# Weights and rows prepared before the barrier between passes, and a bias taken off TensorE in the last graph pass

## The reference, cut to what matters

```python
u = h @ h.T / sqrt(D);  a = softmax(u);  delta = a * adj
attn = delta / (sum(delta) + 1e-10)
hl, hs, hr = h @ wl.T + b_l, h @ ws.T + b_s, h @ wr.T + b_r
ctx = (attn * upper) @ hl + diag(attn)[:, None] * hs + (attn * lower) @ hr
h = relu(layernorm(ctx) * g + beta)
```

## Time and profile before

| | |
|---|---|
| time, median of three runs | 2734.35 us |
| time of the profiled execution | 2734.95 us |
| its span, first to last instruction | 2733.2 us |
| mean granted TensorE clock | 0.964 |
| TensorE busy | 2471.4 us, 90% |
| VectorE, GpSimd, ScalarE busy | 73%, 72%, 62% |

### The profile page before, as it was taken

How to read it: one execution, slowest core, us unless ns; L and a number is a source line. 1 busy time by engine, 2 the same in 40 slices (tenths; PEclk the granted TensorE clock), 3 DMA queues, 4 the chain that set the end, 5 groups by cost and what they waited for, 6 DMA issues and landing times. The chain is left out here.

```text
span 2733.2 us, 65211 instructions
## 1 busy us (share of the span) xinstructions
PE 2471.4 (90%) x21554; PEld 2108.1 (77%) x21554; DVE 1992.3 (73%) x3475; ACT 1689.4 (62%) x3606; POOL 1969.1 (72%) x2189
## 2 busy tenths in 40 slices
PE   6999999985999999869999968888885999999997
PEld 4888888874877777758888857777774888888886
DVE  4777777773677667668888858888787577777776
ACT  4667666664777777745454445555654576666665
POOL 3888788873777777756666647777775588878786
PEclk9999999997999999979999989999997999999998
DMA  7222223115233332172333163333324222232211
GB/s 128 62 71 70 70 65 73 44 50 101 69 84 80 79 81 67 55 129 63 75 73 69 39 120 75 92 79 79 79 70 91 53 69 71 68 72 68 59 46 50
DMA packets 320602, 200.71 MB, mean 73 GB/s; under 512 B 243426, under 2 KB 320484, under 8 KB 320484
## 3 DMA queue, kind: packets, MB, share of 16 engines
q1 hardware_dynamic: 320484, 199.21, 31.6%
HBM read 136.22 MB, written 62.91 MB: 73 GB/s over the span
## 5 line engine op out<-in xcount | busy, mean ns | idle before, releaser
L1179 PE MATMUL l_ps_h<-l_w,l_hT 128*128 128x384 f32 x3456 | 672.0, 347 | 2.3 <-issue 2.3
L457 PE MATMUL l_ps_p<-l_xT,l_w 128*128 128x512 f32 x2304 | 598.3, 407 | 83.3 <-POOL l_xT L379 76.8
L1179 PEld LDWEIGHTS l_ps_h<-l_w,l_hT 128*128 128x128 f32 x3456 | 614.9, 193 | 63.3 <-issue 54.0
L457 PEld LDWEIGHTS l_ps_p<-l_xT,l_w 128*128 128x128 f32 x2304 | 426.3, 191 | 179.8 <-DVE l_w L733 51.7
L784 DVE TENSOR_REDUCE l_st<-l_pr 128x12 f32<-128x768 f32 x192 | 182.9, 953 | 348.7 <-ACT l_pr L663 348.7
L396 POOL TENSOR_TENSOR l_pr<-l_sc,l_st 128x768 f32<-128x768 f32 x192 | 285.1, 1485 | 172.2 <-DVE l_st L777 172.2
L1261 ACT ACTIVATE l_hlr<-l_ps_h 64x384 f32<-64x384 f32 x512 | 248.8, 486 | 196.8 <-PE l_ps_h L1179 190.0
L354 POOL TENSOR_TENSOR v<-v,l_bvs 128x768 f32<-128x768 f32 x192 | 356.2, 1855 | 0.0
L1106 POOL TENSOR_TENSOR l_hlr<-l_hlr,l_sides 128x768 f32<-128x768 f32 x128 | 246.7, 1928 | 125.6 <-ACT l_hlr L1261 125.4
L451 PE MATMUL l_ps_p<-l_w,l_xT 128*128 128x384 f32 x1584 | 312.6, 342 | 15.7 <-ACT v L622 14.8
L451 PEld LDWEIGHTS l_ps_p<-l_w,l_xT 128*128 128x128 f32 x1584 | 272.6, 188 | 25.3 <-ACT v L622 18.8
(11 more groups left out here) (138 smaller groups left out, 4383.6 us busy)
## 6 DMA issues: line engine op xcount, KB each, us to landing
rows<-l_yo SPq DMA_DIRECT2D x256, 192.0 KB, 1.9
l_xa<-rows SPq DMA_DIRECT2D x256, 192.0 KB, 4.3
l_xr<-rows SPq DMA_DIRECT2D x192, 192.0 KB, 2.4
l_xa<-in_x SPq DMA_DIRECT2D x64, 192.0 KB, 4.3
l_xr<-in_x SPq DMA_DIRECT2D x64, 192.0 KB, 2.3
out<-l_yo SPq DMA_DIRECT2D x64, 192.0 KB, 1.9
l_edge<-in_adj SPq DMA_DIRECT2D x80, 128.0 KB, 2.4
raw<-in_L_gnn_Wq SPq DMA_DIRECT2D x12, 144.0 KB, 4.9
```

What stands on the lines that cost most here:

```text
L457: last = nc.tensor.matmul(bank[:, :], W[m][:, l, t, o * P:(o + 1) * P], rows[:, r, t, :], start=c + t == 0, stop=c == 2 and t == KT - 1)
L1179: last = nc.tensor.matmul(ps_h[m][:, :D], hT[gpar][:, l, t, s * P:(s + 1) * P], W[m][:, r, t, :], start=c + t == 0, stop=not (ends and m = ...
```

## The change

1. Weights, row buffers and their semaphores are shared by the passes. A `Feed` object tells each pass where in the running counts it begins. In the last group of an attention pass, or over the last two groups of a graph pass, the streams also turn and split the next pass's 9 weight tiles; the rows of the next pass's first two groups (`g` = 16 and 17) are loaded and turned as if the loop went on, as far as its lookahead reaches. The first graph pass writes into a second set of weight tiles. l0 still prepares its own at its start.
2. The buffer of turned rows in attention passes is doubled.
3. In l0 and l3 the minimum comes after `low_part`.
4. In l1 one VectorE instruction takes the place of the three of ScalarE that normalise a row.
5. The second graph pass does SELF as the first does (`by_matmul = False`), and its stream has `attention` step 3 first in unit 3.

```diff
@@ attention_pass, VectorE
                 nc.vector.tensor_reduce(st[b][:, 0, :], sc[b][:, :, :], AX.X, ALU.max).then_inc(dve_mx, 1)
+
+            def softmax_min(n, s):
+                b = s % 2
                 if wo:
                     nc.vector.tensor_reduce(st[b][:, 1, :], sc[b][:, :, :], AX.X, ALU.min).then_inc(dve_mn, 1)
...
+            def normed(n, count, b):
+                if not inside(n, units) or wo:
+                    return
+                dve.wait_ge(pool_rs, n + 1)
+                dve.wait_ge(dve_mv, n + 1)
+                if counted(16 * count):
+                    dve.wait_ge(s_out[b], 16 * count)
+                nc.vector.tensor_scalar(yo[b][:, :], res[b][:, :], ln[b][:, 6:7], ln[b][:, 9:10], ALU.subtract,
+                                        ALU.mult).then_inc(ready_y, 1)
...
                     softmax_max(n, par, s)
                     low_part(n - 2, s % 2)
+                    softmax_min(n, s)
+                    normed(n - 3, count, 1 - s % 2)
                     if s == 2:
                         edges(i + 1, pair + (1 if par else 0), 1 - par)
                     softmax_sum(n, s)
                     for t in ((0, 1), (2,), (), ())[s]:
                         rows_turned(i + 2, par, t)
+                    if nxt and isinstance(i, int) and i == groups - 1:
+                        if s:
+                            for step in range(KT * (s - 1), KT * s):
+                                weight_low(nxt, step, next_bank(step))
+                        else:
+                            dve.wait_ge(act_v, units)
+                        if s < 3:
+                            for step in range(KT * s, KT * (s + 1)):
+                                weight_turned(nxt, step, next_bank(step), 3)
...
@@ digcn_pass
+    by_matmul = False
...
+        def next_step(i, s):
+
+            j = (i - groups + 2) * UNITS + s if isinstance(i, int) else -1
+            return () if j < 0 else (7, 8) if j == 7 else (j,)
...
@@ digcn_pass, ScalarE
                     left_right(n, b, RIGHT)
+                    for step in next_step(i, s):
+                        weight_high(step)
                     standardise(n - 2, b)
                     normed(n - 4, pair * 4 + 2 * par + s // 2 - 2, b)
-                    if ends:
+                    if by_matmul:
                         act.wait_ge(pe_h, 3 * n + 3)
...
@@ digcn_pass, VectorE
+                    for step in next_step(i, s - 1) if s else next_step(i - 1, UNITS - 1):
+                        weight_low(step)
+                    if s == 3:
+                        attention(i + 1, 1 - par, 3)
+                    itself(n - 1, 1 - b)
                     if ends:
                         context(n - 1, *before)
-                    itself(n - 1, 1 - b)
                     if s == 3:
-                        attention(i + 1, 1 - par, 3)
                         attention(i + 1, 1 - par, 4)
...
                         rows_turned(i + 2, par, s - 2)
+                    for step in next_step(i, s):
+                        weight_turned(step)
...
+    feeds = [Feed(0, x, w0, True, shared.W, 0, 0, 0), Feed(1, kept[0], w1, False, shared.W, 1, 6, 6),
+             Feed(2, kept[1], w2[0], True, shared.W, 1, 6, 6), Feed(3, kept[2], w2[1], True, None, 2, 5, 3),
+             Feed(4, kept[3], w3, True, shared.W, 3, 5, 3)]
```

More of the change, by code:

```diff
@@ L185, in attention_pass @@
         a = Pass(nc, ctx, tag)
-        W = [a.sb(f"w{m}", [P, 2, KT, D], F32R) for m in range(NM)]
+        W = me.W
+        rb, wb = me.rows_base, me.w_base
         ident, raw, s_raw = shared.ident, shared.raw, shared.s_raw
@@ L647, in _ @@
                     rows_high(1, 1, pos - 2)
-            for step in range(3 * KT, steps):
-                weight_high(step)
+            if wo:
+                for t in range(KT):
+                    output_weight_high(t)
             def probs_T(n, b):
@@ L676, in normed @@
             def normed(n, count, b):
-                if not inside(n, units):
+                if not inside(n, units) or not wo:
                     return
@@ L855, in _ @@
             edges(0, 0, 0)
-            for step in range(3 * KT, steps):
-                weight_low(step)
+            if wo:
+                for t in range(KT):
+                    output_weight_low(t)
             ni = [0]
@@ L907, in digcn_pass @@
         loaded = list(shared.loads)
[L908 to L909 removed]
+        own = None if by_matmul else a.sb("own", [P, D])
+        if by_matmul:
             pick = shared.pick
@@ L1412, in itself @@
             def itself(n, b):
-                if ends or not inside(n, units):
+                if by_matmul or not inside(n, units):
                     return
@@ L1471, in inner_norm @@
                                                op0=ALU.mult, op1=ALU.add).then_inc(dve_o, 1)
-            if ends:
+            if by_matmul:
                 nc.vector.memset(bias[:, :].bitcast(F32), 0.0).then_inc(c_zero, 1)
-            weights(LEFT)
             dve.wait_ge(c_mask, masks)
-            for t in range(KT):
-                rows_turned(0, 0, t)
-            weights(RIGHT)
-            attention(0, 0, 0)
-            weights(SELF)
-            for step in range(1, 5):
+            for step in range(5):
                 attention(0, 0, step)
-            rows_turned(1, 1, 0)
-            rows_turned(1, 1, 1)
             dve.wait_ge(s_small, 16 * n_small)
-            if ends:
-                dve.wait_ge(act_w, steps + 1)
+            if by_matmul:
+                dve.wait_ge(c_row, 2)
                 nc.vector.tensor_tensor(bias[32:33, :], brow[32:33, :], bround[32:33, :].bitcast(F32),
@@ L1520, in _ @@
             over_groups(dve, groups, group)
+            for step in next_step(groups - 1, UNITS - 1):
+                weight_low(step)
             itself(units - 1, 1)
```

337 lines of the change are left out of this document (178 added, 159 removed).

## The result

The changed kernel takes 2753.68 us (2750.67 to 2756.05, 4 runs) where the kernel before takes 2734.51 (2733.89 to 2736.66, 4 runs) on the same chip: ratio 1.0067, interval 1.0052 to 1.0082. It is 19 us slower. I had forecast 22 us faster; what came is rival B, priced at 2758.

A forecast was written before the change was run, and what follows sets the result against it. TensorE was taken to pace the first graph pass and nearly l0, a VectorE-TensorE loop the second graph pass, GpSimd's sum to delay VectorE in l1. Terms -17.0 - 11 + 11 - 6 = -23 took 2734.95 to 2712 us; 8-in-10 range 2670 to 2745.

The forecast's parts named there:

- rival B: Second graph pass: SELF's new wait and slowed TensorE give 33.4 us a group, +40 for -6, kernel 2758; chance 0.13.
- part 5: Second graph pass, steady part: 30.3 us a group against 30.7, -6 us in all, bounds -35 and +40.
- I add 0.6 us for that: Second graph pass, per group: allowance for SELF of unit 3 waiting for `itself` behind `wide`, transposition behind SELF.
- VectorE's own need: Second graph pass, rival B: VectorE's bad window kept, 26.1 + 2.8 + 2.1 = 31.0 us a group.
- Part 1: Starts of l1 to l3: TensorE starts about 0.2 us behind each barrier, giving back 48.2 us, bounds 35 and 53.
- part 2: Last groups before the barriers: moved work costs 10.3 in l0, 9.4 in l1, 1.0 and 10.5 in graph passes, 31.2 us.
- rival C: Moving is not saving: tails cost 40 to 43 us, l1's normalising 20, kernel about 2733; chance 0.13.
- l0's contention: l0's last group: first of each three weight splits starts together with GpSimd's multiplication, 3 x 1.06 = 3.2 us.
- The nothing that I charged for ScalarE's high part: First graph pass's end: ScalarE's high part waits behind VectorE's turn; charged 0, up to 8 us if that fails.
- Part 3: l0 and l3, minimum behind `low_part`: TensorE's wait for the low part goes, -11 us, bounds 0 and -23.
- Part 4: l1, normalising on VectorE: new instruction meets GpSimd's, 0.7 a group, +11 us, bounds -8 and +31.

The follow-up runs named there:

- f1_graph_only: The kernel before with only the edit to the second graph pass; 2761.25 us against 2733.66 before.
- g1: f3 with the weights of l1, the first graph pass and l3 turned and split at the start of their own pass; 2693.32 us.
- h2: g1 with 9 extra matmuls ahead of the transposition in unit 3 of the second graph pass; 2680.36 us.
- e3: The changed kernel with only the preparation across barriers and the doubled row buffer kept, the rest as before; 2725.36 us against 2733.44 before.
- f3: e3 with the minimum placed behind `low_part` in l0 and l3; 2710.60 us.
- h0: The changed kernel with l3's weights turned and split at the start of l3; 2751.13 us against 2735.01 before.
- g3: The kernel before with only the minimum placed behind `low_part` in l0 and l3; 2720.74 us against 2732.84 before.
- e1: The changed kernel with the bias matmul and ScalarE's scaled copy back in the second graph pass; 2723.58 us against 2733.44 before.
- f4: e1 with l1's normalising back on ScalarE; 2719.44 us.

## Why the prediction was wrong, point by point

**The step that failed is part 5's "I add 0.6 us for that", SELF of unit 3 waiting for `itself` behind `wide`.** I had the path right in words (the transposition stands behind SELF, SELF behind `itself`, `itself` behind `wide`) and rival B gave its price: 1.7 us of SELF, 33.4 a group. Measured: 32.8. The 0.6 was no row. What it stood for is VectorE's wait for the context product, and that measured 15.1 us in the six groups from 1729.3 to 1926.1, 2.5 a group. In the prediction's own terms the group is 24.8 + 2.8 + 2.1 + 0.6 = 30.3; over these six it is 27.5 busy, 2.8 in gaps and 2.5 waited, 32.8. So 1.9 of the 2.5 missing are the wait and 0.6 is VectorE busier than I had added up. Worked out from rows, as an estimate, the new path gives nearly the same: the whole of `itself` and SELF, 0.55 and 3.25 us from the rows above, less the context, now behind `wide`, 1.4 us in the timeline of before (its three instructions, 1877.77 to 1879.13), is 2.4 more a group, where 2.1 was measured. `f1_graph_only` gives the size of the error by itself: +27.6 us for part 5, forecast -6, 34 of the 42 us by which the kernel missed. Of the 2.1 us a group lost against before, filling the wait gave 1.3 back (32.85 to 31.55 in the mean, 20.8 us in the kernel) and swapping the two calls all of it (30.7). The 1.3 are not the change's own, though: the old form gained 1.2 by the same means (g1 to h2). The order makes the longer path and the longer wait; the clock that falls behind a wait is a price that both orders pay. Rival B had named both, the longer path and TensorE "slowed after a long wait"; it had the mechanism and a chance of 0.13. Its wait was right too (2.4, measured 2.5); it took VectorE's own need as 31.0, measured 30.3. My reason against it, that VectorE has other work in that time, was beside the point: the waiting engine was TensorE, and a loop over two engines is long while both have room.

**Part 1, starts, 48.2.** Within 0.2 us as forecast, and l1 to l3 start on time. The table under part 2 shows that e3 also keeps it: 49 us by the 12th unit. In the changed kernel the second graph pass doesn't keep it: against f1 its 12th unit comes only 2.8 us earlier, forecast 10.0. In `g1_weights_late` three starts were given up in part and lost less than they had gained: the first product of l1 comes 7.7 us behind the barrier, in the first graph pass TensorE waits 3.3 us in all for weights, in l3 the first product comes 3.2 us behind the barrier.

**Part 2, ends, 31.2.** Too small. Each pass can be cut in three at two of its 64 units, by the start of one VectorE instruction that comes once in a unit (the scaled logits in attention passes, the context in graph passes). For `e3_prep_only`, which is preparation alone, against before (one profile each):

| us, e3 less before | l0 | l1 | graph 1 | graph 2 | l3 |
|---|---|---|---|---|---|
| barrier to 12th unit | +0.4 | -19.0 | -8.3 | -10.2 | -12.1 |
| 12th to 55th unit | -0.6 | -0.1 | +0.2 | -8.9 | +0.1 |
| 55th unit to the end | +11.9 | +11.7 | +4.3 | +21.4 | -0.3 |
| charged for the end | 10.3 | 9.4 | 1.0 | 10.5 | 0 |

The starts give 49, the ends take 49. Moving was not saving at all, more so than rival C had it (40 to 43), and the 8.1 us that e3 gains come from a place for which the prediction has no term: the middle of the second graph pass, whose groups take 29.8 us in e3 and 30.8 before. In the changed kernel the ends come nearer to the charge: the second graph pass's is 10.6 longer than f1's, and all four together cost some 39. l0's contention was priced well: the changed kernel's three bursts of three take 2.33, 2.77 and 3.57 us against 3 x 0.55 undisturbed, 3.7 more in all where I had charged 3.2:

```profile
602.98 2.33 DVE L761 TENSOR_TENSOR w<-raw,w 128x384 fp32r<-128x384 f32 x3
614.47 2.77 DVE L761 TENSOR_TENSOR w<-raw,w 128x384 fp32r<-128x384 f32 x3
625.18 3.57 DVE L761 TENSOR_TENSOR w<-raw,w 128x384 fp32r<-128x384 f32 x3
```

The nothing that I charged for ScalarE's high part standing behind VectorE's turn was wrong as well, though not in the place where I looked: it cost TensorE 13.1 us in the second graph pass's end in f3, where ScalarE still carries the own projection, and by h0 hardly anything in the changed kernel.

**Part 3, -11.** Right: -12.1 alone. But TensorE's wait for the low part did not go, as I had said; it is 8.3 us in the window where it was 11.3:

```profile
PE l_ps_y L550 <- DVE l_oT L853: 8.3, 13, 1.0
```

What I had charged, VectorE's wait for TensorE's logits (5.2 us in that window before), is 2.1 in g3 and 0.5 in the changed kernel, and the middle of l0 (12th to 55th unit) is 4.5 us shorter in g3, 0.42 a group. Shown is the size; that this wait is the mechanism is argued, for VectorE's wait for exp fell as well, from 112.3 to 99.7.

**Part 4, +11.** It costs 4.1. The direction and the mechanism were right: the new line takes 1.47 us in the median (57 instances), six times the 0.244 us of the free one in the earlier trace rows, which has 256 values to this one's 384.

```profile
L880 DVE TENSOR_SCALAR l_yo<-l_res,l_ln x57: 971/1471/1525, 690.1 to 1129.8; 128x384 f32<-128x384 f32 x57
```

Nearly all of it hides in VectorE's wait for exp, which falls from 100.6 us in 670 to 1130 before to 34.2, so a group grew by 0.4 us (31.12 to 31.54), not 0.7. That l1 as a whole came out near its forecast is partly luck: its end cost 2.3 us more than charged, part 4 7 us less. The rule of the Trainium skill that I had cited (SBUF — State Buffer, Who interferes with whom: a one-input operation in a two-port mode and a GpSimd one shut each other out) agrees: this line is slow in every instance, while `itself`, whose projection comes from PSUM, takes 0.52 to 0.55 us.

**The sum.** e3, part 3 and part 4 give -8.1 - 14.8 + 4.1 = -18.8; e1, which has them all and the new order of `wide`, measures -9.9, f3 to f4's 8.8 between. From there VectorE's take-out behind `wide` brings +29, and the changed kernel measures +19.2.

Open: why the second graph pass runs 28.7 to 30.6 us a group in e3 and f3 and 30.5 to 30.9 before, with the same order. Its turned rows had two buffers before as well, so the doubling in the attention passes isn't it; the way in which the pass starts and where its buffers lie changed, and no run parts them.

## What to carry to other kernels

When an edit makes engine A wait for an instruction that engine B issues behind the result A needed so far, put on the path everything that A runs between that wait and its next product for B, in full durations, and at the slow clock where rows show it behind such a wait; that B has room does not make the path short. The cheapest cure is order: what is ready first goes first. Work moved ahead across a barrier has to be counted at both ends: here all of it cost what it gave (49 and 49 us), and keeping only rows and one pass's weights ahead was 17 us better than all. The place to look for its price is every queue that it is put in, not only the busiest engine's.

## What the hardware showed that I had not expected

That adding work to TensorE makes a kernel faster by 20.8 and 13 us: a wait of 4.6 to 4.9 us is followed by matmuls at a granted clock of 0.50, and one of 2.34 us by 18 matmuls in 4.89 us in place of 3.38, with a granted clock of 0.67 over those 5.2 us:

```profile
1795.16:1800.40 5.24, 5.24 (x22) 5.03 (x22) 3.47 (x8) 1.99 (x4) 1.99 (x6) 0.67 0.24 75
```

Not every such wait does it. Three groups on, in the same profile of g1, a wait of 2.41 us is followed by 18 matmuls in 3.41 us, at a granted clock of 1.00:

```profile
1885.43 0.66 PE L1235 MATMUL l_ps_a<-ident,l_wide 128*128 128x128 f32 x4 [2.41 <-DVE l_wide L1482]
1886.37 3.41 PE L1251 MATMUL l_ps_h<-second,xT 128*128 128x384 f32 x18 [0.28 <-issue]
```

So behind a short wait as much as two thirds of its length can be lost again (1.7 us behind 2.34), or nothing, and no run here shows what decides.
